# Two normalised convolutions on one core: part of the intermediate's load goes to SyncE's queue, TensorE's waits move a unit ahead, halo copies move from two to three units ahead

## What is computed

```python
def _gn(v, G=4, eps=1e-5):                 # per image and group of 2 channels
    ...
    return ((g - m) / jnp.sqrt(s + eps)).reshape(v.shape)

x = x + _L0_conv_ref(_gn(x), L0_conv_weight, L0_conv_bias)   # 3x3, padding 1, 8 -> 8 channels
x = x + _L1_conv_ref(_gn(x), L1_conv_weight, L1_conv_bias)
return x
```

## Time and profile before

| | |
|---|---|
| time, median of 3 runs (lowest, highest) | 4213.01 us (4202.11, 4214.97) |
| the profiled execution's own time | 4238.59 us |
| span of the profiled execution | 4236.8 us |
| mean granted TensorE clock | 0.978 |
| TensorE busy | 3712.5 us, 88% |
| VectorE, ScalarE, GpSimd busy | 2026.7, 1763.8, 1363.6 us |
| moved by DMA | 1435 MB, mean 339 GB/s |
| SyncE's queue (1 MB tiles) / ScalarE's (loads) / GpSimd's (stores) | 268.45 / 627.30 / 536.96 MB |

### The profile page before, as it was taken

One profiled execution on the slowest core, in us unless ns is written; L12 is line 12 of the kernel. 1 busy time (PEld: TensorE's weight loads), 2 busy tenths in 40 slices (PEclk: granted clock), 3 DMA queues, 4 the chain that ended last, 5 costly groups with the idle time before them and its releaser, 6 DMA issues.

```text
span 4236.8 us, 87949 instructions
## 1 busy us (share of the span) xinstructions
PE 3712.5 (88%) x33232; PEld 1551.0 (37%) x33232; DVE 2026.7 (48%) x3110; ACT 1763.8 (42%) x1381; POOL 1363.6 (32%) x1829
## 2 busy tenths in 40 slices
PE   0087877898889999998889999999999999999999
PEld 0032322353333333353333333345564333343333
DVE  6866666565564444445556344444445222332222
ACT  0032222343334555533333555544443555555554
POOL 0011111111113545521111444441211555555555
PEclk9999898999999999999999999999999999999999
DMA  9989999999999999999999999999999999999997
GB/s 323 392 290 392 387 390 380 354 379 379 380 383 303 343 368 379 338 346 381 376 376 351 303 350 368 337 287 373 357 357 317 283 293 288 282 273 292 289 279 226
DMA packets 367108, 1435.02 MB, mean 339 GB/s; under 512 B 49888, under 2 KB 50016, under 8 KB 334176
## 3 DMA queue, kind: packets, MB, share of 16 engines
q10 hardware_dynamic: 176736, 627.30, 48.4%
q0 software_dynamic: 153344, 536.96, 33.5%
q1 hardware_dynamic: 36864, 268.45, 16.9%
HBM read 895.64 MB, written 536.87 MB: 338 GB/s over the span
## 4 chain that ended last, share of the span: by engine, by line
PE 56%; ACTq 12%; issue 12%; DMA 11%; DVE 6%; ACT 1%; POOL 1%; POOLq 0%; DVEq 0%; SPq 0%
PE conv L632 56%; ACTq L479 12%; DMA out_dram<-out_tile 8%; DMA stat_tile<-x_dram 2%; DVE bn_x L681 2%; ACT out_tile L465 1%; DVE out_tile L708 1%; DVE bn_mid L691 1%; POOL x_tile L405 1%; DMA mid_dram<-out_tile 1%; DVE mv_mid L719 1%; POOL out_dram L385 0%; DVEq L681 0%; DVE mv_x L713 0%; POOLq L385 0%
## 5 line engine op out<-in xcount | busy, mean ns | idle before, releaser
L632 PE MATMUL conv<-x_tile,wts 64*64 64x512 f32 x32832 | 3694.7, 600 | 281.2 <-ACT out_tile L465 190.0
L632 PEld LDWEIGHTS conv<-x_tile,wts 64*64 64x64 f32 x32832 | 1530.7, 135 | 2426.2 <-issue 2363.6
L465 ACT ACTIVATE out_tile<-conv,bias 128x1024 f32<-128x1024 f32 x688 | 729.1, 1111 | 1351.2 <-PE conv L632 749.6
L691 DVE BATCH_NORM_STATS2 bn_mid<-out_tile 128x512 f32 (+1 forms) x1376 | 849.5, 680 | 886.1 <-ACT out_tile L465 885.9
L708 DVE TENSOR_SCALAR out_tile<-conv,bias 128x1024 f32<-128x1024 f32 x340 | 436.4, 1283 | 1253.9 <-PE conv L632 1093.9
L371 POOL DMA_DIRECT2D mid_dram<-out_tile x680 | 344.7, 508 | 1712.2 <-ACT out_tile L465 1658.8
L470 ACT ACTIVATE out_tile<-conv,bias 128x1024 f32<-128x1024 f32 x344 | 383.5, 1115 | 831.9 <-PE conv L632 690.0
L508 ACT ACTIVATE x_tile<-x_tile 16x2048 f32<-16x2048 f32 x340 | 648.7, 1908 | 56.7 <-issue 37.4
L681 DVE BATCH_NORM_STATS2 bn_x<-stat_tile 128x512 f32 (+1 forms) x1024 | 629.1, 678 | 49.6 <-DMA stat_tile<-x_dram 49.4
L405 POOL COPY x_tile<-x_tile 16x2048 f32<-16x2048 f32 x340 | 639.8, 1882 | 1.6
L385 POOL DMA_DIRECT2D out_dram<-out_tile x680 | 349.9, 516 | 899.1 <-DVE out_tile L708 830.3
(11 more groups left out here) (62 smaller groups left out, 115.7 us busy)
## 6 DMA issues: line engine op xcount, KB each, us to landing
x_tile<-x_dram ACTq DMA_DIRECT2D x680, 512.0 KB, 22.7
stat_tile<-x_dram SPq DMA_DIRECT2D x256, 1024.0 KB, 9.9
out_dram<-out_tile POOLq DMA_DIRECT2D x680, 384.0 KB, 7.8
mid_dram<-out_tile POOLq DMA_DIRECT2D x672, 384.0 KB, 9.4
x_tile<-mid_dram ACTq DMA_DIRECT2D x340, 640.0 KB, 6.5
x_tile<-mid_dram ACTq DMA_DIRECT2D x344, 128.0 KB, 8.7
mid_dram<-out_tile POOLq DMA_DIRECT2D x8, 416.0 KB, 10.0
x_tile<-x_dram ACTq DMA_DIRECT2D x8, 256.0 KB
```

The costliest lines, as they stand in the source:

```text
L465: last = act.activation(out_tile[0:parts, slot, i], conv[0:parts, bank, i], ACT.Identity, bias=bias0[0:parts, win.parity, int(unit.last), ...
L632: last = nc.tensor.matmul(to, weights, x_tile[HALF * half:HALF * (half + 1), slot, middle, c + kw:c + kw + BANK], start=(kw == 0), stop=(k ...
L691: last = dve.bn_stats(bn_mid[0:parts, unit.win.pair % 2, i, bass.ds(unit.n * 2 + h, 1), :] .rearrange("p a b -> p (a b)"), out_tile[0:part ...
```

## The change

1. SyncE issues one of the two loads of a layer 1 unit, that into 16 partitions (last units excepted), in its step u for unit u+8, after a new wait for `conv_done` of u. ScalarE issues the other as before. At the first unit of a layer 1 window SyncE waits for the stores of the intermediate, as ScalarE does.
2. Both halos are copied three units ahead, not two.
3. TensorE's waits for unit u+1 stand in unit u, in its second column half: for load and pads before tap 0, for the halos before tap 1, for the bank before tap 2. In a layer 1 unit (last ones excepted) the wait for the load itself is gone, since the halo copies have waited for it.

```diff
@@ SyncE
+        def load_mid(queue, unit, part, first, rows, done):
+            both = mid[unit.win.image:unit.win.image + 2, bass.ds(first, rows), :]
+            queue.dma_start(x_tile[part:part + rows, unit.slot, :, 1:SIDE + 1],
+                            both.rearrange("n r w -> r n w")).then_inc(done, 16)
...
                 def step(unit, in_loop):
+                    following = unit.after(X_RING)
+                    if following is not None and following.win.layer == 1 and not following.last:
+                        if following.b == 0:
+                            wait_for_mid(sp, following.win)
+                        sp.wait_ge(conv_done, unit.count + 1)
+                        sp.sem_inc(slots_free)
+                        load_mid(sp, following, P - PAIR,
+                                 following.n * OUT_ROWS + (CH + MID_PARTS), PAIR,
+                                 x_loaded[following.slot])
                     if not in_loop and unit.b == HEAD - 1 and win.x_each:
@@ GpSimd
-                    following = unit.after(2)
+                    following = unit.after(3)
                     if following is not None and following.win.layer == 1 and following.b:
                         copy_first_halo(following)
@@ ScalarE
-                load_rows(VALID, first, MID_PARTS, x_loaded[slot])
-                load_rows(P - PAIR, first + MID_PARTS, PAIR, x_loaded[slot])
+                load_mid(act, unit, VALID, first, MID_PARTS, x_loaded[slot])
...
-                    following = unit.after(2)
+                    following = unit.after(3)
                     if following is not None and following.win.layer == 1 and not following.last:
                         copy_second_halo(following)
@@ TensorE
-            def wait_for_bank(earlier):
+            def wait_for_rows(unit):
+                if unit.win.layer == 0 or unit.last:
+                    pe.wait_ge(x_loaded[unit.slot], (unit.turn + 1) * 32)
+                if unit.win.layer == 1 and unit.kind == TOP:
+                    pe.wait_ge(edge_loaded, 16 * (same_layer_before(unit.win) + 1))
+                if isinstance(unit.n, int) and unit.n < X_RING:
+                    pe.wait_ge(pads_written, unit.win.w * X_RING + unit.n + 1)
+                pe.sem_inc(unit_begun)
+            def wait_for_halos(unit):
+                if unit.win.layer == 1 and unit.kind != TOP:
+                    pe.wait_ge(first_halo, halos_through(unit))
+                if unit.win.layer == 1 and not unit.last:
+                    pe.wait_ge(second_halo, halos_through(unit) + 1)
+                pe.sem_inc(unit_begun)
+            def wait_for_bank(unit):
+                earlier = unit.before(2)
+                if earlier is None:
+                    return
                 pe.wait_ge(evicted_a, earlier.count + 1)
                 if earlier.win.layer == 1:
                     pe.wait_ge(evicted_v, earlier.layer_count + 1)
+                pe.sem_inc(unit_begun)
 
             def convolve(unit, read=None):
...
+                following = unit.after(1)
                 for c in range(0, SIDE, BANK):
                     if c and read is not None:
                         pe.wait_ge(*read)
                     for kw in range(KW):
+                        if c and following is not None:
+                            if kw == 0:
+                                wait_for_rows(following)
+                            elif kw == 1:
+                                wait_for_halos(following)
+                            else:
+                                wait_for_bank(following)
```

More of the change, by code:

```diff
@@ L233, in conv_preact_blocks @@
         stat_used = sem("stat_used")
+        slots_free = sem("slots_free")
         edge_loaded = sem("edge_loaded")
@@ L256, in halos_through, with wait_for_mid @@
             return same_layer_before(unit.win) * UNITS + unit.n
+        def load_mid(queue, unit, part, first, rows, done):
+            both = mid[unit.win.image:unit.win.image + 2, bass.ds(first, rows), :]
+            queue.dma_start(x_tile[part:part + rows, unit.slot, :, 1:SIDE + 1],
+                            both.rearrange("n r w -> r n w")).then_inc(done, 16)
+        def wait_for_mid(queue, win):
+            done = next(v.w for v in WINDOWS if v.layer == 0 and v.pair == win.pair) + 1
+            for s in range(RING):
+                queue.wait_ge(stored[s], 32 * len(range(s, done * UNITS, RING)))
+            queue.wait_ge(stored_last, 16 * last_stores(done))
         AGGREGATE, MEAN, VAR, ROOT, WEIGHTS = (TAIL + X_RING + d for d in (0, 4, 5, 6, 7))
@@ L488, in load @@
                     return
[L490 to L493, removed]
                 first = unit.n * OUT_ROWS + CH
                 if unit.last:
-                    load_rows(PAIR, first, PAIR, x_loaded[slot])
-                    load_rows(3 * PAIR, first + PAIR, CH, x_loaded[slot])
+                    load_mid(act, unit, PAIR, first, PAIR, x_loaded[slot])
+                    load_mid(act, unit, 3 * PAIR, first + PAIR, CH, x_loaded[slot])
                     return
                 if unit.kind == TOP:
-                    load_rows(CH, 0, CH, edge_loaded)
-                load_rows(VALID, first, MID_PARTS, x_loaded[slot])
-                load_rows(P - PAIR, first + MID_PARTS, PAIR, x_loaded[slot])
+                    load_mid(act, unit, CH, 0, CH, edge_loaded)
+                load_mid(act, unit, VALID, first, MID_PARTS, x_loaded[slot])
             def copy_second_halo(unit):
@@ L511, in copy_second_halo @@
                                ACT.Identity).then_inc(second_halo, 1)
[L513 to L518, removed]
             def take_root(n):
@@ L536, in step @@
                         if following.b == 0 and following.win.layer == 1:
-                            wait_for_mid(following.win)
+                            wait_for_mid(act, following.win)
                         neighbour = unit.after(1)
@@ L643, in _ @@
             bias_sum(0, 0)
+            wait_for_rows(Unit(WINDOWS[0], 0))
             for win in WINDOWS:
@@ L647, in step @@
                 def step(unit, in_loop):
-                    earlier = unit.before(2)
-                    if earlier is not None:
-                        wait_for_bank(earlier)
                     read = None
```

## The result

| | before | after |
|---|---|---|
| median of 6 runs (lowest, highest), us | 4213.99 (4192.49, 4219.74) | 4187.12 (4183.48, 4197.04) |
| ratio, 95% interval | | 0.9945 (0.9925, 0.9965) |
| the profiled execution's own time, us | 4238.59 | 4186.1 |

The change is faster by 0.55%, 27 us at the median; 62 were forecast.

The account below looks back on a forecast made before the run. Layer 1 was taken as braked by a halo chain as long as its unit, not bandwidth. Terms -28, -11, -15, -10, -6 and +8 gave -62 us: 4176.6 profiled, 4151 by the median; own range 4125 to 4180, wide 4110 to 4200.

Parts of the forecast that it names:

- (e): Loops of windows 2 and 4, ends of 1 and 3: tiles +23.3, -14 and +5, halo slack -20, together -6 us.
- (a): Loops (units 9-64) of windows 6 and 7: halos three ahead bring them near TensorE's own pace, -28 us.
- (b): Units 0-8 of the four layer 1 windows: unit 1's halo can be copied in the previous window, -11 us.
- (c): Units 65-66 behind layer 1 loops: the new slack covers GpSimd's lateness and the clock stays up, -15 us.
- (d): Units 67-85 of layer 1 windows: nearer TensorE's pace, except part of the wait where weights are made, -10 us.
- (f): TensorE's waits a unit ahead: free in layer 1, stops at late layer 0 evictions, +8 us of at most 56.
- the -20 of (e): Loops of windows 2 and 4: the halos' slack gains about half of what the bounds allow, -10 us each.
- the bound of 0: Loops of windows 2 and 4: no gain from the halos' slack if DMA alone sets the pace at today's rate.
- B: Rival, no change: TensorE's ahead waits cost in full, 56 instead of 8 us, giving 4199; chance 0.08.
- C: Rival, no change: mid-unit waits interrupt TensorE, 0.1 us in each of 688 units, +69, giving 4220; chance 0.06.
- A: Rival, slower: SyncE's queue falls behind in windows 2 and 4, 6.9 us a unit, +134, giving 4285; chance 0.08.
- D: Rival, more gain: the slack frees windows 2 and 4 up to 387 GB/s, giving 4119 us; chance 0.08.

## Why the prediction went wrong, step by step

The direction, the place of the gain and the wide range (4110 to 4200) were right; the forecast's own range (4125 to 4180) and the size were not: 62 us forecast, 27 measured. The step that failed is the price of SyncE's part in (e). By the stretches of the two profiled executions:

| step | forecast | measured | from |
|---|---|---|---|
| (a) loops of 6 and 7 | -28 | -30 | 303.8 to 288.6 and 288.5 |
| (b) units 0-8 | -11 | -13 | 49.6 to 46.4, four times |
| (c) units 65-66 | -15 | -15 | window 6 14.7 to 10.7, window 2 15.4 to 15.6, window 4 17.7 to 10.3 |
| (d) units 67-85 | -10 | -10 | window 6 104.6 to 100.9, window 7 100.7 to 98.2, windows 2 and 4 by 1.2 and 2.5 |
| (e) windows 2 and 4 with the ends of 1 and 3 | -6 | +13 | loops +19.2 and +11.5, ends -10.6 and -6.8 |
| (f) and the rest | +8 | +3 | what is left of the span's -52.4, other windows' scatter included |

**Halo chain, (a) to (d).** Right in mechanism, and -68 in the profiled pair where -64 were forecast. That the kernel with the halos alone is also 64 us faster at the median is partly luck: its forecast was -84 with the -20 of (e), and its profiled execution lies 95 us under that of before. The new slack holds the loop's end at full clock: 10.7 us with PEclk 1.00.

**SyncE's part, in (e): the step that failed.** The tiles' late issue was priced at 23.3 - 14 + 5 = +14; alone it costs 13. The 16-partition load was asked only whether it lands in time ("it has the time from u's end to step u+5's copy") and priced at nothing. It does land in time, 7.9 us after issue at the median of units 17 to 64 of window 2:

```profile
x_tile<-mid_dram SPq DMA_DIRECT2D x48, 128.0 KB, 7.9
```

But it costs 36 us, and while it runs the sum of all queues is lower. The loops of windows 2 and 4 took 336.0 us each, where 316 to 330 were forecast. 112 us of window 2's loop at 331 GB/s where 374 would be are 112 x (1 - 331/374) = 13 us, 26 in both windows, which is about the 25 us that their loops are longer with the load; where the other 10 lie was not followed. The Trainium skill ("SBUF — State Buffer", Door 1: The DMA port swizzle) has a rule that bears on it: a transfer reaches only the ports of its own partitions, and 16 neighbouring partitions cover 4 of 16, 32 cover 8. The Trainium skill ("DMA: Bandwidth & Descriptors", Back-pressure in remote DMA) adds, for transfers between cores, that a saturated port holds up the engines behind it. The two runs with 16 and 32 partitions (4185.08 and 4149.79 us) agree with the first of the two; that ports are the way in which it works, no run here shows by itself. Why the same load costs nothing behind the wide one in ScalarE's queue was not separated either; the measured fact is 4144 to 4150 us there.

**The other half of (e), -20 for the slack in windows 2 and 4.** Mis-sized as well. Halos alone leave their loops at 315.7 and 311.6 us, 1 and 13 less than in the profiled execution of before, where 10 each were forecast on top of a cost that is not in this kernel. What holds them are mostly stores: with halos and waits ahead and no load on SyncE, VectorE still waits 131.8 us in 39 waits for a slot's store in units 17 to 64 of window 2:

```profile
DVE out_tile L729 <- DMA out_dram<-out_tile: 131.8, 39, 6.0
```

DMA sets most of the pace there, as the bound of 0 had it.

**Carried over unchanged.** I took the 25.6 us between the profiled execution and the median as a constant. It was not: the profiled pair differs by 52.5, the medians by 27. Terms read off one execution that lies high, in the windows where DMA varies, come out too large; units 9 to 64 of window 3, whose code is the same in both, took 343.7 us in it and 332.3 with the halos alone. So it is luck that the profiled pair's -52 lies near the forecast's -62.

**(f), waits ahead.** Forecast +8, measured nothing: halos alone 0.9849, halos and waits 0.9847 and 0.9837. Intervals of some 11 us to each side do not exclude the 8, but they do exclude the 56 of B and the 69 of C. In the profiled executions window 0's loop took 401.7 us before, 405.2 with the halos alone and 408.1 with SyncE's load alone, all three without the waits ahead, and 411.7 in the change, so a few us may be there. B and C fall by the medians, and C also by window 5's loop, 288.5 us after. A was the right place with the wrong mechanism: the queue did not fall behind. D did not come.

In medians the parts are -64 for the halos, 0 for the waits and +40 for SyncE: -24, against -27 for the change. Each was taken from the one before, so that they add up proves little; that SyncE's load alone, put on the kernel before, costs 41 us is the independent figure. The forecast had -84, +8 and +14. Of the gap SyncE's part makes 26 us and the halos' slack 20, and the waits give 8 back.

The versions that beat both are the change without its SyncE part, 4144 to 4150 us, or the kernel before with `unit.after(3)` alone, 4152; the two are not told apart.

## What to carry to other kernels

Ask of a moved transfer not only whether it lands in time but what it does to the others while it runs: here a small load into few partitions took a tenth off the rate of all queues at once, which cost time where DMA set the pace and none where TensorE did. When a wait moves ahead, move its producer ahead first. And where a chain of copy and store is as long as the step it serves, one step more of distance can stand in for any shortening of the chain: here a 2 became a 3 in two places.

## What the runs showed of the hardware

- A 128 KB load into 16 partitions brings the sum of all queues from 371 to 376 down to 331 to 340 GB/s where it shares its queue with the tiles, and from 375 to 302 alone in its queue; into 32 partitions it leaves it at 388 (386 otherwise). In ScalarE's queue, right behind the wide load into the neighbouring partitions, it costs no time that shows (4144 to 4150 us).
- Six ways to spread the same transfers over two issuing engines span 87 us. Exchanging the engines changes nothing (4231.20 and 4230.69; 4205.44 and 4200.21); which transfers stand in one line changes up to 2%.
- With the loads behind tiles, stores land sooner (11.2 us instead of 17.8 with both loads in ScalarE's queue and the tiles in SyncE's), and the kernel is slower: the line that is late has moved from stores to loads.
